# Constants awaited in parts, expert units of the first and last passes at other places, and a last sum on the vector engine, in a Mamba block between two expert layers

## The chip, the cores and the metric

One core of one Trainium2 chip runs the kernel. The metric is the time of one execution on the device in microseconds (us), the median of three runs. The five engines have their own instruction streams and meet through semaphores only: TensorE (PE; its weight loads are PEld), VectorE (DVE), ScalarE (ACT), GpSimd (POOL) and SyncE (SP), which here only issues DMAs.

## What is computed

32 sequences of 256 tokens with 128 channels pass through a half-weighted expert layer, a Mamba layer and a second half-weighted expert layer, each on a normalised input and added to the residual:

```python
x = x + 0.5 * ffn(layernorm(x))      # 8 experts of 176, top 2 of 8, and a shared expert of 352
x = x + mamba(layernorm(x))
x = x + 0.5 * ffn(layernorm(x))      # the same weights
# mamba, on r = layernorm(x):
xz = r @ W_in + b_in;  x_in, z = split(xz)                    # 256 each
xc = silu(causal_conv4(x_in) + conv_b)
Bm, Cm = split(xc @ W_xp + b_xp);  delta = softplus(xc @ W_dt + b_dt)
h_t = exp(delta_t * A) * h_(t-1) + delta_t * xc_t * Bm_t      # 256 channels x 16 states
y = sum over states of h_t * Cm_t + D_skip * xc
out = layernorm_std(r + (y * silu(z)) @ W_out + b_out)
```

## The kernel before, in words

**Tiles.** The 16 groups (`G`) are two sequences each, 512 tokens (`TG`). Channels lie on the 128 partitions in the Mamba part, so that one state of one group is one scan of 128x1024: `hist` from `decay` and the input term in the PSUM tile `ps_db`, 16 scans (`NS`) to a group, 256 in all (L924). GpSimd multiplies each with the row of C (`prod`, L623), and an accumulating DMA (L640) adds each pair of products to `yacc`; a last one, `fold` (L598), adds its two halves.

**The expert layer** is one pass of 14 units (`NCHUNK`): three of the shared expert (`ORDER` puts them first), then eleven of 128 rows of the experts. A unit is two up matmuls (`ps_h1` L1076, `ps_h2` L1098), a silu on ScalarE (L706), a multiply on VectorE (the gate, L904, with the row of routing weights `wrow` for expert units), a multiply on GpSimd for expert units (the join, L555), and four slots later (`BACK`) its down matmuls into `ps_y` (L1090). Up to seven gated tiles, four silus and four rows of weights are kept; the two PSUM tiles of each kind hold two units. The weight rows go by DMA through DRAM (`store_w`, then two DMAs of SyncE per unit, L418).

**Iterations.** The program is a pipeline over `k` from -2 to 17. Iteration `k` has 32 slots (`SLOTS`). Where group `k` exists, it runs its 16 scans, one per two slots, and beside them the first expert layer of group `k+2`, the front of the Mamba layer of group `k+1` (`lead`: `addy0` to `du`, ending in `bT`, the transposed B rows), the tail of group `k-1` (`fold`, the gating of y, the output projection, the layer norm `stats3` to `ln_add`, the routing of the second expert layer) and the second expert layer of group `k-2`. So iterations 2 to 13 hold 28 units each, iterations 0, 1, 14 and 15 hold 14, and -2, -1, 16 and 17 hold 14 units and no scan.

**What sets the order.** Tables written by hand: `PLAN` gives the slot of each step, `UNIT` the slots of the units, `SP_PLAN` the DMAs of SyncE; `START_PLAN`, `START_UNIT` and `START_SP` do so for `k` below 2 (`FULL`). Each engine walks the same slots and emits its own part of each step, so an engine's instructions stand in slot order and wait in that order. All the small matmul outputs (`xT`, `logits`, `wT`, `in0` to `in3`, `dt`, `xproj`, `cT`, `bT`, `outproj`) share one PSUM bank, `ps_m`, one after the other: a step waits until the one ahead has been copied out.

**Setup.** TensorE first waits for all eight expert weight loads, issued by ScalarE's queue (`experts_loaded`). SyncE issues the first group's x, fifteen constants (`consts_loaded`) and four more x. `prepare()` (VectorE, slot 24 of iteration -2) waits for all fifteen constants; `make_the_rest()` (GpSimd, slot 16) makes eleven small constants, `sel_b` among them, which the row broadcast `row_b` (L1058) needs; `make_edge()` (TensorE, slot 28) makes the edge term of the convolution.

## Time and profile before

| | before |
|---|---|
| median of 3 runs (lowest to highest) | 1839.37 us (1837.52 to 1846.04) |
| the profiled execution | 1839.04 us |
| its span, first to last instruction | 1837.3 us |
| PE / DVE / ACT / POOL busy | 1658.7 / 1478.3 / 1266.2 / 1445.7 us |
| mean granted TensorE clock | 0.959 |
| first matmul / first scan / last scan begin | 18.39 / 133.44 / 1740.03 us |

Busy shares are means over stages with different limits. The start, the sixteen scanning iterations and the end have to be read apart, which the windows do: each gives the busy time of every engine in one stretch.

### The profile page before, as it was taken

The page shows a single profiled execution, that of the slowest core. Times are in us where ns is not written, and L with a number is a line of the kernel's source. Part 1 is how long each engine was busy: PE and PEld are TensorE (multiplying, and loading weights), DVE is VectorE, ACT ScalarE, POOL GpSimd, SP SyncE. Part 2 cuts the span into 40 slices and gives each one's busy share as a digit, 9 for nine tenths or more (in the row PEclk, how much of TensorE's full clock was granted, in tenths as well). Part 3 has the DMA queues.
Part 4 walks back from the last instruction along what each step waited for, and adds up shares of the span by engine and source line. Part 5 has one row for each costly group of instructions (what it writes and reads, how often), then busy time and mean ns, then how long its engine had stood idle before and what let it go on. Part 6 is the DMA issues. An engine that isn't in the chain of part 4 may idle for free.

```text
span 1837.3 us, 24041 instructions
## 1 busy us (share of the span) xinstructions
PE 1658.7 (90%) x7378; PEld 1001.5 (55%) x7378; DVE 1478.3 (80%) x2241; ACT 1266.2 (69%) x2030; POOL 1445.7 (79%) x1366
## 2 busy tenths in 40 slices
PE   5898788999999999999999999999999999958488
PEld 3454445556555555656555555656555555534255
DVE  1438889989798988989798988989898998989732
ACT  2367678787877778776867777786877777665422
POOL 3336869888898988888888888888898888887753
PEclk9998889999999999999999999999999999969599
DMA  6026768687776868686777867777677868767642
GB/s 158 24 87 141 180 150 193 160 205 173 185 184 162 207 156 201 158 194 170 178 184 170 201 158 189 181 187 184 168 190 172 196 156 192 184 152 186 143 104 69
DMA packets 121287, 304.54 MB, mean 166 GB/s; under 512 B 19299, under 2 KB 40518, under 8 KB 106822
## 3 DMA queue, kind: packets, MB, share of 16 engines
q0 software_dynamic: 18432, 125.84, 34.4%
q1 hardware_dynamic: 98406, 174.46, 33.3%
q10 hardware_dynamic: 4320, 2.71, 0.5%
q8 instruction: 58, 0.95, 0.2%
q14 instruction: 71, 0.58, 0.1%
HBM read 167.67 MB, written 5.24 MB: 94 GB/s over the span
## 4 chain that ended last, share of the span: by engine, by line
POOL 43%; DMA 23%; issue 14%; PE 9%; DVE 7%; ACT 1%; SPq 1%; POOLq 0%; ACTq 0%; DVEq 0%
DMA yacc<-prod 19%; POOL prod L623 18%; POOL gated L555 14%; DVE hist L924 4%; DMA crow<-c_rows 3%; POOL yacc L619 2%; PE ps_y L1090 2%; DVE ps_db L876 2%; POOL yacc L640 1%; PE ps_h1a L1076 1%; SPq L418 1%; PE ps_h2a L1098 1%; PE ps_h1b L1076 1%; PE ps_h2b L1098 1%; POOL xres L610 1%
## 5 line engine op out<-in xcount | busy, mean ns | idle before, releaser
L623 POOL TENSOR_TENSOR prod<-hist,crow 128x1024 f32<-128x1024 f32 x224 | 556.5, 2484 | 204.7 <-DVE hist L924 171.0
L1090 PEld LDWEIGHTS ps_y<-down_w,gated 128*128 128x128 f32 (+1 forms) x3584 | 474.0, 196 | 276.4 <-issue 160.1
L924 DVE TENSOR_TENSOR_SCAN hist<-decay,ps_db 128x1024 f32<-128x1024 f32 x256 | 583.3, 2278 | 2.8
L555 POOL TENSOR_TENSOR gated<-gated,silu 128x512 f32<-128x512 f32 x352 | 493.3, 1450 | 74.4 <-DVE gated L904 71.4
L1090 PE MATMUL ps_y<-down_w,gated 128*128 128x128 f32 (+1 forms) x3584 | 491.8, 282 | 58.0 <-POOL gated L555 56.3
L876 DVE TENSOR_TENSOR ps_db<-du,ps_db 128x1024 f32<-128x1024 f32 x256 | 313.2, 1224 | 114.2 <-PE ps_db L1058 112.1
L686 ACT ACTIVATE decay<-delta,a_neg 128x510 f32<-128x510 f32 x512 | 326.8, 709 | 3.7 <-DVE delta L965 2.2
L706 ACT ACTIVATE silu<-ps_h1a 128x512 f32<-128x512 f32 (+1 forms) x224 | 132.9, 593 | 194.8 <-PE ps_h1a L1076 194.6
L1076 PE MATMUL ps_h1b<-xnT,up_w 128*128 128x512 f32 x448 | 236.7, 610 | 3.6 <-ACT silu L706 3.1
L1098 PE MATMUL ps_h2a<-xnT,up_w 128*128 128x512 f32 (+1 forms) x448 | 236.1, 609 | 1.9 <-DVE gated L904 1.9
L1076 PE MATMUL ps_h1a<-xnT,up_w 128*128 128x512 f32 (+1 forms) x448 | 236.4, 609 | 0.0
L1098 PE MATMUL ps_h2b<-xnT,up_w 128*128 128x512 f32 x448 | 232.0, 600 | 1.4 <-DVE gated L904 1.4
L904 DVE TENSOR_TENSOR gated<-ps_h2b,wrow 128x512 f32<-128x512 f32 x192 | 130.7, 681 | 60.3 <-PE ps_h2b L1098 40.2
L706 ACT ACTIVATE silu<-ps_h1b 128x512 f32<-128x512 f32 x224 | 133.0, 594 | 63.6 <-PE ps_h1b L1076 52.1
L686 ACT ACT_TABLE_LOAD x124 | 159.1, 1283 | 2.2
L904 DVE TENSOR_TENSOR gated<-ps_h2a,wrow 128x512 f32<-128x512 f32 x160 | 107.9, 674 | 46.3 <-PE ps_h2a L1098 36.2
L706 ACT ACT_TABLE_LOAD x111 | 142.4, 1283 | 2.0
L1058 PE MATMUL ps_db<-bT,sel_b 96*128 96x512 bf16 x256 | 102.2, 399 | 41.5 <-DVE hist L924 41.4
L1047 PE MATMUL ps_m<-xnT,w_conv 128*128 128x512 f32 (+3 forms) x256 | 118.2, 596 | 0.0
L1076 PEld LDWEIGHTS ps_h1a<-xnT,up_w 128*128 128x128 f32 (+1 forms) x448 | 85.0, 192 | 56.6 <-issue 47.0
L1076 PEld LDWEIGHTS ps_h1b<-xnT,up_w 128*128 128x128 f32 x448 | 79.1, 194 | 64.0 <-issue 37.5
L640 POOL DMA_DIRECT2D yacc<-prod x112 | 101.6, 908 | 1.6 <-issue 1.3
(136 smaller groups left out, 1937.5 us busy)
## 6 DMA issues: line engine op xcount, KB each, us to landing
yacc<-prod POOLq DMA_DIRECT2D x112, 1024.0 KB, 10.0
crow<-c_rows SPq DMA_DIRECT2D x128, 512.0 KB, 5.0
wrow<-w_rows SPq DMA_DIRECT2D x320, 128.0 KB, 6.3
wrow<-w_rows SPq DMA_DIRECT2D x64, 224.0 KB, 7.0
wrow<-w_rows SPq DMA_DIRECT2D x64, 192.0 KB, 6.4
wrow<-w_rows SPq DMA_DIRECT2D x64, 160.0 KB, 2.9
yacc<-yacc POOLq DMA_DIRECT2D x16, 512.0 KB, 7.8
wrow<-w_rows SPq DMA_DIRECT2D x64, 96.0 KB, 2.9
```

The costliest lines, as they stand in the source:

```text
L555: nc.gpsimd.tensor_tensor(gated[:, pos % NGATE, :], gated[:, pos % NGATE, :], silu[:, (pos + NCHUNK * f_parity(of, f)) % NSILU, :], ALU.mu ...
L623: nc.gpsimd.tensor_tensor(prod[:, (pair - 1 + odd) % 2, s % 2, :, :], hist[:, s % 2, :, :], c_all, ALU.mult).then_inc(prod_done, 1)
L640: pool.dma_start(yacc[odd][:], prod[:, (pair - 1 + odd) % 2, :, :, :], accum_op=ALU.add).then_inc(acc_done, 16)
L686: ins = nc.scalar.activation(decay[:, s % NA, half, :, 1:LEN], d[:, :, 1:LEN], ACT.Exp, scale=a_neg[:, half, s:s + 1])
L706: nc.scalar.activation(silu[0:r, (pos + NCHUNK * f_parity(k, f)) % NSILU, :], ps_h1[pos % 2][0:r, :], ACT.Silu).then_inc(silu_done, 1)
L876: nc.vector.tensor_tensor(ps_db[:].rearrange("p (h t) -> p h t", h=HALVES), du[par][:], ps_db[:, TG:2 * TG].unsqueeze(1).to_broadcast([P, ...
L904: nc.vector.tensor_tensor(gated[0:r, pos % NGATE, :], ps_h2[pos % 2][0:r, :], factor, ALU.mult).then_inc(h2_taken, 1)
L924: nc.vector.tensor_tensor_scan(hist[:, s % 2, :, :].rearrange("p h t -> p (h t)"), decay[:, s % NA, :, :, :].rearrange("p h b t -> p (h b ...
L1047: nc.tensor.matmul(acc[:, :, late:LEN], w_conv[:, tap, half * P:(half + 1) * P], now[:, :, 0:LEN - late], start=(tap == PAD), stop=False)
L1076: nc.tensor.matmul(ps_h1[pos % 2][0:r, :], up_w[:, 0, j * P:j * P + r], xnT[f][:], start=True, stop=True).then_inc(h1_full, 1)
L1090: ins = nc.tensor.matmul(ps_y[:, t * C:(t + 1) * C], gated[0:rd, posd % NGATE, t * P:(t + 1) * P], down_w[0:rd, jd, :], start=(posd == 0 a ...
L1098: nc.tensor.matmul(ps_h2[pos % 2][0:r, :], up_w[:, 1, j * P:j * P + r], xnT[f][:], start=True, stop=True).then_inc(h2_full, 1)
```

## The change

The tables are split by iteration. `PLANS[k]`, `UNITS[k]` and `SP_PLANS[k]` hold iterations -2, -1, 0, 14 (`G - 2`), 15, 16 and 17; the others keep their tables. An entry `name@1` belongs to the next iteration's work, `(f, pos, 1)` likewise for a unit.

- *Constants.* TensorE no longer waits for all expert weights at its start. The gate weights are awaited at the first `logits0`, the shared up weights at unit 0, the experts' up weights at unit 3, the down weights at the first down matmul. SyncE, not ScalarE, issues the down weights, right behind the first x. Behind the up weights' arrival it issues the five constants of the convolution (`conv_loaded`), and the other ten only in slot 8, behind the rows of the first four experts. `prepare()` becomes three steps: `taps_w`, `taps_b` and, an iteration later, `bias_parts`. `make_sel` stands in slot 2 on GpSimd. A silu of one element on ScalarE (`warm`) comes ahead of everything.
- *First passes.* The first pass (group 0) takes one unit per slot from slot 6. The second (group 1) has units 0 to 5 in iteration -2, units 6 and 7 in iteration -1, and units 8 to 13 in slots 0 to 5 of iteration 0, whose own 14 units follow from slot 7. The front of group 0 begins in iteration -2.
- *Last passes.* The last three passes begin one iteration sooner: seven units of group 13's pass in iteration 14 and seven in 15, eight units of group 14's in 15 and six in 16, and all of group 15's in 16. `ln_scale`, `ln_shift` and `ln_add` of the last group share slot 7.
- *Last sum.* For the last group, the seventh accumulate and the fold are left out. VectorE adds the second half of `yacc` and the two last products itself (`sum`).

```diff
+    PLANS[-2] = {
+        0: ["stats0"], 1: ["scale0"], 2: ["make_sel", "norm0"], 4: ["xT0"], 5: ["logits0", "rcopy0"], 6: ["route0", "tilt0"],
+        7: ["weights0", "wT0"], 12: ["taps_w"], 13: ["taps_b"], 15: ["stats0@1"], 16: ["scale0@1"], 17: ["norm0@1"],
...
+    UNITS[-2] = {6 + pos: (0, pos) for pos in range(NCHUNK)}
+    UNITS[-2].update({s: (0, pos, 1) for pos, s in enumerate((21, 22, 24, 26, 28, 30))})
+    SP_PLANS[-2] = {
+        7: ["store_w0", "w0:0", "w0:1", "w0:2", "w0:3"], 8: ["consts", "load:1"], 10: ["w0:4", "w0:5", "load:2"],
...
+    UNITS[-1] = {2: (0, 6), 4: (0, 7)}
...
+    UNITS[0] = {pos - 8: (0, pos, -1) for pos in range(8, NCHUNK)}
+    UNITS[0].update({s: (0, pos) for pos, s in enumerate((7, 8, 10, 13, 15, 18, 21, 22, 23, 24, 25, 27, 29, 31))})
...
+    UNITS[G - 2] = {s: unit for s, unit in UNIT.items() if unit[0] == 1}
+    UNITS[G - 2].update({s: (1, pos, 1) for pos, s in enumerate((21, 23, 25, 28, 29, 30, 31))})
...
+    UNITS[G - 1] = {s: (1, 7 + pos) for pos, s in enumerate((0, 2, 4, 6, 8, 10, 12))}
+    UNITS[G - 1].update({s: (1, pos, 1) for pos, s in enumerate((21, 22, 24, 27, 28, 29, 30, 31))})
...
+    UNITS[G] = {pos - 8: (1, pos) for pos in range(8, NCHUNK)}
+    UNITS[G].update({11 + pos: (1, pos, 1) for pos in range(NCHUNK)})
...
             load(0, 0, 0)
-            sp.wait_ge(x_loaded, 16)
+            full = HS // P
+            const(down_w[:, ECHUNK:ECHUNK + full, :], Ws3[0:full * P, :].rearrange("(j p) c -> p j c", p=P), down_loaded)
+            const(down_w[0:LAST, NCHUNK - 1, :], Ws3[full * P:HS, :], down_loaded)
+            const(down_w[:, 0:ECHUNK, :], W3.rearrange("e h c -> (e h) c").rearrange("(j p) c -> p j c", p=P), down_loaded)
+            sp.wait_ge(up_loaded, 16 * N_UP)
...
-                            if s % 2:
+                            if s % 2 and not (final(k + 1) and pair == PAIRS):
                                 accumulate(k, odd, pair)
...
+            act.wait_ge(pads_zero, 1)
+            nc.scalar.activation(warm[:], decay[:, 0, 0, 0, 0:1], ACT.Silu)
...
+                        elif step == "sum":
+                            dve.wait_ge(acc_done, 16 * (PAIRS * it - 1))
+                            dve.wait_ge(prod_done, NS * it)
+                            y_all = yacc[nxt][:, 0, :, :].rearrange("p h t -> p (h t)")
+                            left = prod[:, (PAIRS - 1 + nxt) % 2, :, :, :]
+                            for n, term in enumerate((yacc[nxt][:, 1, :, :], left[:, 0, :, :], left[:, 1, :, :])):
+                                if n:
+                                    dve.wait_ge(summed, n)
+                                nc.vector.tensor_tensor(y_all, y_all, term.rearrange("p h t -> p (h t)"), ALU.add
+                                                        ).then_inc(summed, 1)
...
             pe.wait_ge(consts_made, MADE_FIRST)
-            pe.wait_ge(experts_loaded, 16 * N_EXPERTS)
...
+                        if n == 0:
+                            pe.wait_ge(shared_loaded, 16 * 2)
+                        if n == NCHUNK - ECHUNK:
+                            pe.wait_ge(up_loaded, 16 * N_UP)
```

TensorE around the first scans, before. `ps_db<-bT,sel_b` is the row broadcast ahead of a scan, `ps_h` a unit's up matmuls, `ps_y` its down matmuls, and `bparts` the transpose for `bT`:

```order
L1037 MATMUL ps_m<-ident_bf,bparts 96x128 x4
L1076 MATMUL ps_h1a<-xnT,up_w 128x512
L1090 MATMUL ps_y<-down_w,gated 128x128 x4
L1098 MATMUL ps_h2a<-xnT,up_w 128x512
L1076 MATMUL ps_h1b<-xnT,up_w 128x512
L1098 MATMUL ps_h2b<-xnT,up_w 128x512
L1076 MATMUL ps_h1a<-xnT,up_w 128x512
L1090 MATMUL ps_y<-down_w,gated 128x128 x4
L1098 MATMUL ps_h2a<-xnT,up_w 128x512
L1076 MATMUL ps_h1b<-xnT,up_w 128x512
L1098 MATMUL ps_h2b<-xnT,up_w 128x512
L1058 MATMUL ps_db<-bT,sel_b 128x512
```

The same place after:

```order
L1136 MATMUL ps_m<-ident_bf,bparts 96x128 x4
L1248 MATMUL ps_m<-xnT,w_in 128x512
L1194 MATMUL ps_y<-down_w,gated 128x128 x4
L1248 MATMUL ps_m<-xnT,w_in 128x512
L1194 MATMUL ps_y<-down_w,gated 128x128 x4
L1157 MATMUL ps_db<-bT,sel_b 128x512
L1178 MATMUL ps_h1a<-xnT,up_w 128x512
L1202 MATMUL ps_h2a<-xnT,up_w 128x512
L1178 MATMUL ps_h1b<-xnT,up_w 128x512
L1202 MATMUL ps_h2b<-xnT,up_w 128x512
L1157 MATMUL ps_db<-bT,sel_b 128x512
```

Four units' up matmuls stood between the transpose for `bT` and the first row broadcast; now two small input matmuls and two down groups do, and the units stand behind it.

VectorE behind the last scan (`hist`), before, down to the first step of the gating of y (`xconv,d_c,yacc`):

```order
L924 SCALAR_TENSOR_TENSOR hist<-decay,ps_db 128x1024
L904 TENSOR_TENSOR gated<-ps_h2a,silu 128x512
L904 TENSOR_TENSOR gated<-ps_h2b,silu 128x512
L904 TENSOR_TENSOR gated<-ps_h2a,silu 96x512
L904 TENSOR_TENSOR gated<-ps_h2b,wrow 128x512
L904 TENSOR_TENSOR gated<-ps_h2a,wrow 128x512
L904 TENSOR_TENSOR gated<-ps_h2b,wrow 128x512
L904 TENSOR_TENSOR gated<-ps_h2a,wrow 128x512
L985 SCALAR_TENSOR_TENSOR yacc<-xconv,d_c,yacc 128x512
```

And after:

```order
L1016 SCALAR_TENSOR_TENSOR hist<-decay,ps_db 128x1024
L996 TENSOR_TENSOR gated<-ps_h2a,wrow 128x512
L996 TENSOR_TENSOR gated<-ps_h2b,wrow 128x512
L996 TENSOR_TENSOR gated<-ps_h2a,wrow 128x512
L1090 TENSOR_TENSOR yacc<-yacc 128x1024
L1090 TENSOR_TENSOR yacc<-yacc,prod 128x1024 x2
L996 TENSOR_TENSOR gated<-ps_h2b,wrow 128x512
L1102 SCALAR_TENSOR_TENSOR yacc<-xconv,d_c,yacc 128x512
```

Seven gates stood there; now three gates, the three adds and one more gate stand there.

SyncE's queue behind the first store of routing weights (`w_rows`), before:

```order
L403 DMA w_rows<-bounce 8x512
L418 DMA wrow<-w_rows 64x512 x2
L418 DMA wrow<-w_rows 48x512
L418 DMA wrow<-w_rows 80x512
L418 DMA wrow<-w_rows 96x512
L418 DMA wrow<-w_rows 32x512
L418 DMA wrow<-w_rows 64x512 x2
L418 DMA wrow<-w_rows 16x512
```

And after:

```order
L548 DMA b_dt_c<-L_attn_b_dt 128x2x1
L548 DMA w_xp<-L_attn_W_xp 128x2x32
L548 DMA b_xp_b<-L_attn_b_xp 128x32
L548 DMA a_log<-L_attn_A_log 128x2x16
L548 DMA d_c<-L_attn_D_skip 128x2x1
L548 DMA b_out_r<-L_attn_b_out 3x128
L548 DMA w_out<-L_attn_W_out 128x2x128
L548 DMA alpha_b<-L_attn_alpha 128x128
L548 DMA beta_b<-L_attn_beta 128x128
L470 DMA xres<-L_attn_x 128x4x128
L512 DMA wrow<-w_rows 16x512
L512 DMA wrow<-w_rows 112x512
```

Before, the constants stood far ahead of this place. Now ten of them (`w_dt`, right ahead of the rows shown, and the nine at their top) stand behind the rows of the first four experts and ahead of the fifth's (the pair of 16 and 112 partitions), with the next group's x.

## Rows read from the trace of the kernel before

**Rows 1.** Windows: stretch; us; busy of PE, PEld, DVE, ACT, POOL; clock, DMA share, GB/s.
```profile
18.39:133.40 115.01, 103.66 (x415) 60.66 (x415) 35.82 (x97) 50.91 (x87) 44.41 (x49) 0.94 0.23 68
133.40:217.60 84.20, 66.26 (x253) 37.68 (x252) 72.40 (x86) 64.11 (x94) 61.49 (x51) 0.88 0.65 157
217.60:311.90 94.30, 75.42 (x296) 44.84 (x297) 82.44 (x125) 67.53 (x111) 75.73 (x74) 0.87 0.69 163
415.70:520.40 104.70, 100.10 (x463) 60.79 (x462) 92.30 (x140) 79.11 (x128) 89.60 (x85) 1.00 0.75 180
1561.90:1654.20 92.30, 70.27 (x302) 42.06 (x301) 80.56 (x102) 61.62 (x94) 77.26 (x68) 0.84 0.70 167
1654.20:1740.00 85.80, 56.33 (x216) 33.37 (x215) 72.28 (x84) 45.76 (x71) 66.88 (x59) 0.76 0.71 169
1740.00:1837.30 97.30, 83.85 (x369) 52.06 (x367) 31.19 (x70) 24.19 (x48) 41.79 (x44) 0.90 0.35 87
```

**Rows 2.** Chain of waits, start of the program: start us, us, what.
```profile
7.30 11.00 DMA down_w<-L_ffn_W
18.39 1.10 PE ps_m L1037 x4
```

**Rows 3.** Timeline, ScalarE: start us, us, engine, line, operation [idle before <- releaser].
```profile
7.85 1.28 ACT L673 ACT_TABLE_LOAD   x1 [7.85 <-POOL nbias L544]
9.14 1.65 ACT L673 ACTIVATE xn<-xres,nbias,rstd 128x128 f32<-128x128 f32 x4
```

**Rows 4.** Chain of waits, first expert pass.
```profile
38.19 1.96 POOL sel_b L509
...
52.22 6.07 issue
```

**Rows 5.** Timeline, around the first scan.
```profile
131.28 0.38 PE L1058 MATMUL ps_db<-bT,sel_b 96*128 96x512 bf16 x1
...
133.44 2.28 DVE L924 TENSOR_TENSOR_SCAN hist<-decay,ps_db 128x1024 f32<-128x1024 f32 x1
```

**Rows 6.** Chain of waits, last expert pass, at full clock.
```profile
1808.76 0.86 PE ps_h1a L1076 x2
1809.62 0.89 PE ps_y L1090 x8
```

**Rows 7.** Timeline, SyncE's queue: first and last of ten constants' loads.
```profile
7.66 0.50 SPq L448 DMA_DIRECT2D w_dt<-L_attn_W_dt  x1
...
14.44 0.43 SPq L448 DMA_DIRECT2D beta_b<-L_attn_beta  x1
```

**Rows 8.** Tile wrow, VectorE: what its gate multiplies waited for (us, times).
```profile
  DMA wrow<-w_rows: 30.1, 19
```

**Rows 9.** Timeline, end of the last scans.
```profile
1740.03 2.29 DVE L924 TENSOR_TENSOR_SCAN hist<-decay,ps_db 128x1024 f32<-128x1024 f32 x1
...
1745.72 0.89 POOL L640 DMA_DIRECT2D yacc<-prod  x1 [0.25 <-POOL carrier_p L632]
...
1761.17 0.75 DVE L985 SCALAR_TENSOR_TENSOR yacc<-xconv,d_c,yacc 128x512 f32<-128x512 f32 x1 [3.73 <-DMA yacc<-yacc]
```

**Rows 10.** Line 969, an operation with both inputs in SBUF: ns min/median/max.
```profile
L969 DVE TENSOR_TENSOR du<-delta,xconv x16: 1198/1968/2976, 121.2 to 1647.5; 128x1024 f32<-128x1024 f32 x16
```

**Rows 11.** Chain of waits, from output projection to last expert pass.
```profile
1768.24 0.70 DVE rtok L917
...
1790.55 0.20 DVE logit L944
...
1794.95 1.71 PE ps_h1a L1076 x2
```

**Rows 12.** Page, parts 5 and 6: groups of instructions and DMA issues.
```profile
L623 POOL TENSOR_TENSOR prod<-hist,crow 128x1024 f32<-128x1024 f32 x224 | 556.5, 2484 | 204.7 <-DVE hist L924 171.0
...
L555 POOL TENSOR_TENSOR gated<-gated,silu 128x512 f32<-128x512 f32 x352 | 493.3, 1450 | 74.4 <-DVE gated L904 71.4
...
wrow<-w_rows SPq DMA_DIRECT2D x320, 128.0 KB, 6.3
```

758 lines of the change are left out of this document (405 added, 353 removed), and 23 rows, old and new, of the table SP_PLANS.

## The prediction

> **What bounds the kernel now.** I read the windows of busy time first, cut at the starts of the scans [rows 1]. Each stretch from 133.40 to 1740.00 us is one iteration of 16 scans, and the row for 415.70 to 520.40 stands for the twelve full ones, iterations 2 to 13: 104.7 us, in which TensorE is busy 100.1 at a granted clock of 1.00. The full iterations are bound by TensorE. Those at the ends are not: iteration 0 takes 84.2 us with TensorE busy 66.3 and VectorE 72.4, iteration 14 takes 92.3 with 70.3 and 80.6, iteration 15 takes 85.8 with 56.3 and 72.3. They have room on TensorE. Before the first scan lie 133.4 us, after the start of the last one 97.3 us, and there it is TensorE again, on the expert layers [rows 1]. So the ends have matrix work with no scan beside it, and the iterations next to them have scans with too little matrix work. The span is 1837.3 us, the execution 1839.04; the 1.7 us around it stay.
>
> The chain of waits says what else the ends hold. The first matmul starts at 18.39 us, released by the last of the weight loads, issued at 7.30 [rows 2]; the normalised rows it transposes were ready at 10.8, after a table load of 1.28 [rows 3]. In the first expert pass a 2 us piece of making `sel_b` on GpSimd stands in the chain (the last of three, behind a memset), and later 6.07 us of "issue" while VectorE works on the prepared constants [rows 4].
>
> **Start, to the first matmul.** PE now waits for the 14 small constants and the norm; the gate weights are awaited at `logits0`, the others where first read. ACT issues five loads and not eight, so its queue is free before the norm's inputs come, and the table load is done while it waits. With the norm's four activations (1.65) following at about 7.5, PE starts at 9.2: 9.2 us earlier, with 1.3 of it from the table. The down weights go out on the other queue at the same time as the up weights; they are 0.9 MB of the 2.7 MB that landed by 18.4 and are read only four units later, so I take no wait for them. If I am wrong on that, the first matmuls stall until what used to be 18.4, and at most 5 of the 9.2 are lost, since five units' work then lies ahead of them.
>
> Here a page speaks against it. The table switch took 1.28 us in the trace, and the ACTIVATE follows 0.01 behind it [rows 3]. The Trainium skill, ScalarE: Activation LUTs, section "What ACT_TABLE_LOAD costs", gives 1.283 us plus a drain of 1.38, about 2.66 per switch. After the change four switches lie between `sp_exp` and the first decays; by the page each would cost an estimated 1.38 us more than in the row, 5.5 in all, and the kernel would take 1820. The row has no such gap, and the sum goes by the row.
>
> **Start, to the first scan.** I count the work in PE's list. Before, between the first matmul and the first row broadcast (`row_b`, 131.28, [rows 5]), it holds 28 pairs of up matmuls and 24 groups of down matmuls: all 14 units of two passes. After, it holds 22 pairs and 22 groups, since six units of the second pass now come behind `row_b`. A matmul pair is 0.86 us, two to a unit, and a down group 0.89 at full clock [rows 6]: 6 x 1.72 + 2 x 0.89 = 12.1 us less. PE was busy 103.7 of the 115.0 us from 18.39 to 133.40 [rows 1], of which some 1.9 are behind `row_b`; that leaves 103.7 - 1.9 - 12.1 = 89.7. The idle part was 11.3. The `sel_b` stall (GpSimd now makes it in slot 2, between the norm and the first weights, where it waits) and the constants' stall (two short steps now, with the output bias put behind `du`) go, about 4 and 5 us. New idle comes: the rows of expert 4 stand on the SP queue behind ten constants, whose issue took 7.2 us (7.66 to 14.87, [rows 7]; 1 us left over on PE); the second pass's first three units fill only part of the wait for addy0, stats2, scale2 and norm2 (3 us); `dt0`, `dt1`, `xproj`, `cT`, `bT`, `in2`, `in3` pass through the one bank `ps_m` with fewer units between them, each waiting for ScalarE's copy (5 us); and ScalarE ends with `in3`, a table load and two decays after `row_b` (3 us, where the first scan stood 2.2 us behind `row_b` [rows 5]). So 12 us idle including that end, less clock saved by shorter gaps, which I take as 5 us of the lower 0.94 grant: 9.2 + 89.7 + 12 - 5 = 106. **First scan at 106 us, 27.4 earlier**; with the stalls halved or doubled, and none or all of the clock, 99 to 114.
>
> **The units that move into scans.** What a unit costs inside an iteration is read from two rows: iteration 1 has 14 units in 94.3 us and a full one 28 in 104.7, with the same tail and front steps [rows 1], so (104.7 - 94.3) / 14 = 0.74 us each, which is about one gate multiply on VectorE. Iteration 0 gets six more (20 units), iteration 14 seven more (21), iteration 15 one more (15). At 0.74 that is 4.4, 5.2 and 0.7. The other bound is the whole 2.61 us of PE work per unit [rows 6] where PE is late: 15.7, 18.3, 2.6. I take values near the lower end because PE has 18 to 30 us free in each, and add for placement. In iteration 0 six units come one per slot in the first three scans, about 5.8 us of PE work per scan against an average spacing of 84.2 / 16 = 5.3. In iterations 14 and 15 the rows for the moved units are stored right behind `next_c0` or `c7` on the SP queue, and a gate that waits for a row has a scan behind it on VectorE; the whole run had only 30.1 us of that wait in 19 places [rows 8]. **+6.5, +6 and +2 us.** Iterations 1 to 13 have the same list on each engine; +0.
>
> **The end.** Before, the last accumulate is issued at 1745.72, the fold behind it, and the gating of y starts at 1761.17, which is 21.1 us after the last scan began at 1740.03 [rows 9]. After, VectorE adds three 128x1024 tensors itself. Such an add with both inputs in SBUF took 1.20 at least, 1.97 in the middle and 2.98 at most [rows 10]: 3.6 to 8.9, taken as 5.9, since GpSimd still multiplies beside it. The sixth accumulate has landed by about +5, since the seventh could be issued at 1745.72. But `sum` stands behind three unit gates (positions 6 to 8), and their matmuls begin on PE only behind the last row broadcast, two units and a half of 2.61 us and more at the lower clock: it starts at +7.5, ends at +13.4, and the four multiplies of the y gates (0.75 each at least, [rows 9]) with two unit gates take about 7 us if they too are held up: +20.5. The output projection then ends at +23, against 1768.24, that is +28.2 [rows 9, 11]: 5.2 us won of the 16 that the accumulate and the fold held.
>
> From there to the logits' arrival on VectorE took 22.3 us (1768.24 to 1790.55) [rows 11]. The layer norm's three GpSimd multiplies no longer have unit multiplies between them: 2.2 less. The units now start behind the logits and not behind the routing: 1790.55 to 1794.95, 4.4 us [rows 11], less 0.7 for the transpose that they now carry. The expert rows then come at about +13 after the logits where PE wants them at +11; the two-deep buffers take that up. Sum: 5.2 + 2.2 + 3.7 = 11.1, **end 11 us shorter**, with 6 to 15 as bounds (the adds at 8.9 and a stall on the rows; the adds at 3.6).
>
> **Sum.** 1839.0 - 27.4 + 6.5 + 6 + 2 - 11.1 = 1815.0 us. The profiled execution is 0.3 us below the median of the three runs, so this stands for the median too.
>
> **Rivals.**
> (a) *The moved units hide better, and PE runs without the clock losses.* Their low price holds (10.3 instead of 14.5), the first scan comes at 101, the end is 13 shorter: 1839 - 32.4 + 10.3 - 13 = 1804. For it: 18 to 30 us of free TensorE time. Against: VectorE is at 72 to 81 of 84 to 92 us there.
> (b) *The iterations that receive them behave like full ones, or worse.* Then iterations 0 and 14 go towards 100 and 104, +16 and +12, and 15 +4, first scan at 108: 1839 - 25 + 32 - 11 = 1835; in its milder half, 1827. For it: GpSimd multiplies 1.45 us per expert unit beside its 2.48 per scan [rows 12], and the accumulate DMA chain paces iteration 0.
> (c) *Slower: rows late in front of scans.* Fifteen units with expert rows are gated in iterations 0, 14 and 15 in places of the scans where none was. If each gate waits for its row, the scan behind it is held. A row's landing took 6.3 us in the median [rows 12]. The change decides for slower from a mean wait of 24 / 15 = 1.6 us; at half a landing, 3.1 us, it costs 47 and gives 1862. Against it: 19 waits in 352 such gates before.
> (d) *The start does not do what it says*: weights shared over two queues land no earlier and PE stands at 18 as before. First scan 9 later, 1824; it lies in the range.
>
> A second rule bears on the end. Adds of this form took between 1.20 and 2.98 us [rows 10]. The Trainium skill, SBUF — State Buffer, section "Who interferes with whom", has a VectorE instruction with two SBUF inputs fully blocked while a GpSimd one that reads SBUF runs. By it, each of the three adds could stand behind a whole multiply, an estimated 7 to 9 us for the sum, and the kernel 1 to 3 us later than the forecast, inside the range.
>
> **How the numbers follow.** The forecast, 1815, has 0.56; (a) 0.20; (b) 0.19; (c) 0.05; (d) is a part of the forecast's spread. The range takes in the forecast with its own bounds (about 1805 to 1826), most of (a) below and the milder half of (b) above: 1800 to 1830. A measurement of this kernel can tell some 0.5% from no change, 9 us. Faster by more is below 1830: the forecast, (a), and two thirds of (b), 0.89. Within 0.5%: the rest of (b) and a little of (c), 0.08. Slower: 0.03.
>
> **What would show it.** In the profile after: the first matmul at 9 to 10 us; no `sel_b` in the chain; the first scan at 99 to 114; iterations 0, 14 and 15 at 90.7, 98.3 and 87.8; the twelve full ones unchanged; three adds on VectorE at 1.2 to 3 us each, starting 7 to 8 us after the last scan's start; 86 us from there to the end. It is wrong if the first matmul waits for a weight, if gates wait on `wrow` for far over 30 us in all, if TensorE's grant in iteration 0 falls further below 0.88, or if full iterations change though their lists do not.

## The result, and the profile after

The changed kernel takes **1854.37 us** (median of 9 runs, 1849.88 to 1857.21), the kernel before 1840.83 (9 runs, 1834.86 to 1846.04). The ratio is 1.0074, with a 95% interval of 1.0059 to 1.0088: slower by 0.7%. The forecast was 1815.0 with a range of 1800 to 1830, so the time lies outside it and on the other side of no change. The profiled execution has a span of 1851.0 us, 13.7 more than the 1837.3 of before.

The windows of busy time, cut at the starts of the scans as in [rows 1], say where they are. Columns: stretch in us; its length; busy time of PE, PEld, DVE, ACT and POOL with their instructions; granted clock, DMA share, GB/s.

```profile
9.39:102.63 93.24, 86.28 (x365) 52.42 (x366) 33.65 (x92) 37.41 (x72) 34.32 (x36) 0.98 0.35 96
102.63:210.37 107.74, 79.30 (x311) 43.86 (x309) 74.43 (x91) 75.99 (x109) 68.21 (x57) 0.92 0.53 133
210.37:303.24 92.87, 78.18 (x288) 46.00 (x289) 80.95 (x125) 66.21 (x108) 74.77 (x74) 0.80 0.71 165
1555.82:1677.64 121.82, 95.17 (x362) 55.56 (x361) 83.60 (x109) 71.47 (x107) 80.09 (x72) 0.82 0.58 142
1677.64:1767.09 89.45, 53.83 (x206) 31.09 (x206) 72.36 (x84) 43.83 (x69) 64.59 (x56) 0.79 0.68 156
1767.09:1851.00 83.91, 69.24 (x318) 45.22 (x317) 33.52 (x68) 18.50 (x39) 41.02 (x39) 0.91 0.22 67
```

Beside the forecast's terms (us; an iteration runs from the start of its first scan to the next iteration's):

| stretch | before | after | difference | forecast |
|---|---|---|---|---|
| first matmul | 18.4 | 9.4 | -9.0 | -9.2 |
| start to first scan | 133.4 | 102.6 | -30.8 | -27.4 |
| iteration 0 | 84.2 | 107.7 | **+23.5** | +6.5 |
| iteration 1 | 94.3 | 92.9 | -1.4 | 0 |
| iterations 2 to 13 | 1250.0 | 1252.5 | +2.5 | 0 |
| iteration 14 | 92.2 | 121.9 | **+29.7** | +6 |
| iteration 15, to the last scan | 85.8 | 89.4 | +3.6 | +2 |
| last scan to the end | 97.3 | 83.9 | -13.4 | -11.1 |
| sum | 1837.3 | 1851.0 | +13.7 | -24.0 |

(The first row is part of the second.) The start and the end gained more than forecast. Two iterations lost 53 us where 12.5 had been expected: iteration 0, with 20 units, is longer than a full iteration with 28 (103 to 107), and iteration 14, with 21 units, is the longest of the run.

How far such a length can be read is seen from the experiments below, since many of them share tables. The ten profiles with the changed kernel's tables for iteration 14 gave 119.8 to 121.9 us for it; the seven with its tables for iteration 0 gave 107.7 to 109.8; the stretch after the last scan gave 83.9 to 85.7, the first scan 101.9 to 104.7, and the twelve full iterations together 1247 to 1254. Differences under 2 us in one stretch (3 at the first scan) are not read as effects. Only `e1`, `e2`, `e5`, `e11` and `e16` were executed more than once (4 to 10 times); each of the others is one execution, and is read by its stretches.

**The start** did what it was to do. The timeline, ScalarE and TensorE (start, length, engine, line, operation; in brackets the idle time before it and what ended it):

```profile
3.35 1.28 ACT L758 ACT_TABLE_LOAD   x1 [3.35 <-issue]
4.64 0.20 ACT L758 ACTIVATE warm<-decay 128x1 f32<-128x1 f32 x1
7.60 1.65 ACT L771 ACTIVATE xn<-xres,nbias,rstd 128x128 f32<-128x128 f32 x4 [2.75 <-POOL nbias L645]
```
```profile
9.39 1.09 PE L1136 MATMUL ps_m<-ident,xn 128*128 128x128 f32 x4 [9.39 <-ACT xn L771]
```

The table load of [rows 3] lies ahead of the norm, TensorE starts on the norm and not on a weight as in [rows 2], and the two stalls of [rows 4] are gone from the chain.

**Iteration 14** shows two long waits of VectorE, each with a scan behind it. Its timeline:

```profile
1606.01 2.28 DVE L1016 TENSOR_TENSOR_SCAN hist<-decay,ps_db 128x1024 f32<-128x1024 f32 x1
1615.55 0.06 DVE L950 MEMSET carrier_s<- 128x1 f32 x1 [7.26 <-POOL xres L710]
...
1618.46 2.28 DVE L1016 TENSOR_TENSOR_SCAN hist<-decay,ps_db 128x1024 f32<-128x1024 f32 x1
...
1633.18 1.23 DVE L971 TENSOR_TENSOR ps_db<-du,ps_db 128x1024 f32<-128x1024 f32 x1 [4.69 <-PE ps_db L1157]
...
1659.71 1.20 DVE L1071 TENSOR_TENSOR du<-delta,xconv 128x1024 f32<-128x1024 f32 x1
1669.34 0.69 DVE L996 TENSOR_TENSOR gated<-ps_h2b,wrow 128x512 f32<-128x512 f32 x1 [8.42 <-DMA wrow<-w_rows]
```

The first: the statistics of the second norm (`stats1`) now stand in slot 17 with the layer norm's last add (`ln_add`), which GpSimd reaches behind two unit multiplies and a scan product; the scan of slot 18 waits behind them, 12.5 us from one scan to the next. The last: the first gate that reads a row of routing weights waits 8.4 us for it, again with a scan behind it. SyncE's queue at that place:

```profile
1644.98 0.32 SPq L486 DMA_DIRECT2D c_rows<-bounce  x1
1658.57 0.32 SPq L491 DMA_DIRECT2D crow<-c_rows  x1
1658.94 0.46 SPq L497 DMA_DIRECT2D w_rows<-bounce  x1
```
```profile
1653.89 0.59 ACT L846 ACTIVATE bounce<-ps_m 8x512 f32<-8x512 f32 x1 [1.19 <-PE ps_m L1136]
```

ScalarE had the weights in `bounce` by 1654.5. Their store (`w_rows<-bounce`) went out at 1658.94, behind the load of the next group's first C rows (`crow`), which waits for the products of scan 13.

**Iteration 0** has the same two kinds. Its longest gap, 13.9 us from scan 6 (141.27) to scan 7 (155.16), on VectorE and TensorE:

```profile
141.27 2.29 DVE L1016 TENSOR_TENSOR_SCAN hist<-decay,ps_db 128x1024 f32<-128x1024 f32 x1
149.37 1.23 DVE L971 TENSOR_TENSOR ps_db<-du,ps_db 128x1024 f32<-128x1024 f32 x1 [5.81 <-PE ps_db L1157]
154.55 0.69 DVE L996 TENSOR_TENSOR gated<-ps_h2b,wrow 128x512 f32<-128x512 f32 x1 [3.96 <-DMA wrow<-w_rows]
155.16 2.28 DVE L1016 TENSOR_TENSOR_SCAN hist<-decay,ps_db 128x1024 f32<-128x1024 f32 x1
```
```profile
143.72 1.09 PE L1136 MATMUL ps_m<-ident,x1n 128*128 128x128 f32 x4 [4.06 <-ACT bounce L846]
144.59 1.92 PE L1178 MATMUL ps_h1b<-xnT,up_w 128*128 128x512 f32 x2
146.30 1.10 PE L1202 MATMUL ps_h2b<-xnT,up_w 128*128 128x512 f32 x2
147.23 1.88 PE L1146 MATMUL ps_m<-xnT,w_conv 128*128 128x512 f32 x4
148.95 0.38 PE L1157 MATMUL ps_db<-bT,sel_b 96*128 96x512 bf16 x1
```

The row broadcast for scan 7 (`ps_db<-bT,sel_b`, 148.95) stands on TensorE behind the transpose of the second norm, and that waits for ScalarE. In the kernel before this chain stood in slots 5 to 8; it could not stay there, because the six units of the second pass now end in slot 9 and the second norm needs their sum.

### The profile page after: what moved, and what is told of

The parts are those of the page before. It is cut to its first block, busy times and chain, and to the rows that moved or that the text cites. A ratio compares the mean times of both kernels' runs of the same rounds, so it can differ in the third digit from the quotient of the medians.

```text
span 1851.0 us, 24043 instructions
## 1 busy us (share of the span) xinstructions
PE 1665.0 (90%) x7378; PEld 1005.1 (54%) x7378; DVE 1484.5 (80%) x2244; ACT 1266.1 (68%) x2031; POOL 1445.5 (78%) x1362
## 4 chain that ended last, share of the span: by engine, by line
POOL 44%; DMA 17%; issue 15%; PE 14%; DVE 5%; ACT 4%; POOLq 0%; SPq 0%; DVEq 0%; ACTq 0%
POOL prod L723 18%; DMA yacc<-prod 15%; POOL gated L654 13%; PE ps_y L1194 4%; POOL yacc L719 3%; DVE hist L1016 2%; PE ps_h1a L1178 2%; PE ps_h2b L1202 2%; PE ps_h1b L1178 2%; PE ps_h2a L1202 2%; POOL yacc L740 2%; DMA wrow<-w_rows 1%; PE ps_m L1146 1%; DVE ps_db L971 1%; POOL xres L710 1%
## 5 line engine op out<-in xcount | busy, mean ns | idle before, releaser
L1202 PE MATMUL ps_h2b<-xnT,up_w 128*128 128x512 f32 x448 | 237.3, 612 | 9.5 <-DVE gated L996 9.4
L1157 PE MATMUL ps_db<-bT,sel_b 96*128 96x512 bf16 x256 | 101.7, 397 | 44.2 <-DVE hist L1016 44.0
L1178 PEld LDWEIGHTS ps_h1a<-xnT,up_w 128*128 128x128 f32 (+1 forms) x448 | 85.1, 193 | 62.5 <-issue 45.9
```

Source lines behind the costliest of these rows:

```text
L1178: nc.tensor.matmul(ps_h1[pos % 2][0:r, :], up_w[:, 0, j * P:j * P + r], xnT[f][:], start=True, stop=True).then_inc(h1_full, 1)
L1202: nc.tensor.matmul(ps_h2[pos % 2][0:r, :], up_w[:, 1, j * P:j * P + r], xnT[f][:], start=True, stop=True).then_inc(h2_full, 1)
```

## The experiments

**Theories.** U: the moved units make the two iterations long, by their work and their own waits. T: the steps that had to move with them do (router, norms, transposes), because in their new slots one engine waits for another with a scan queued behind it.

### One move undone at a time

`e1_late_back` puts the last passes back, `e2_first_back` the second pass and iteration 0 (here and below `...` stands for lines left out):

```
+    for table, full in ((PLANS, PLAN), (UNITS, UNIT), (SP_PLANS, SP_PLAN)):
+        table[G - 2] = table[G - 1] = full
...
+    UNITS[G] = {pos: (1, pos) for pos in range(NCHUNK)}
+    UNITS[G].update({16 + pos: (1, pos, 1) for pos in range(NCHUNK)})
...
```
```
+    UNITS[-1] = {1 + n: (0, 6 + n) for n in range(8)}
...
+    PLANS[0], UNITS[0], SP_PLANS[0] = START_PLAN, START_UNIT, START_SP
```

> The changed kernel with its last three expert passes put back: iterations 14 and 15 take the tables of the full ones again (14 units each), and all 14 units of the pass before the last stand behind the last scan, beside the sum and the output projection. The two profiles put +29.7 us on iteration 14 and +3.7 on iteration 15. Both theories expect iterations 14 and 15 at about 92 and 86 us, 33 shorter. What is open is the end (83.9 us in the changed kernel, 97.3 before): if its gain came from the chain (sum on VectorE, no multiplies between the layer norm's steps), it stays at 84 to 88 and the kernel takes about 1822; if it came from the eight units that no longer stand there, it goes back to 95 to 98 and the kernel takes 1832 to 1835.

> The changed kernel with the second pass's six units back ahead of the first scan and iteration 0 with its old tables (14 units, old steps); loads and the early front stay. Expected by both theories: first scan about 12 us later than 102.6, so near 115; iteration 0 back from 107.7 to 84 to 86; iteration 14 unchanged at about 122. Kernel about 1854 + 12 - 23 = 1843. If iteration 0 stays over 95, its length is not from its own tables but from what the start leaves behind (a colder clock, accumulates).

Measured: `e1_late_back` 1821.41 us, ratio to before 0.9907 (0.9890 to 0.9924). Iterations 14 and 15 took 91.5 and 85.8, and the end 87.6: with all 28 units behind the last scan it is still 9.7 shorter than before. The end's gain comes from its chain; moving eight units away from it was worth at most 4 us there (87.6, and 85.9 in a later kernel, against 83.9 to 85.7), and cost 34 in iterations 14 and 15. `e2_first_back` 1839.78 us, ratio 1.0011 (0.9999 to 1.0023): first scan at 116.0, iteration 0 at 85.9. The first move alone wins 13.4 and costs 21.8.

### Units against steps

`e3_first_units` takes the six units out of iteration 0 and leaves its other tables; `e4_late_units` takes the seven out of iteration 14:

```
+    UNITS[-1] = {1 + n: (0, 6 + n) for n in range(8)}
...
+    UNITS[0] = {s: unit for s, unit in UNITS[0].items() if len(unit) == 2}
...
```
```
+    UNITS[G - 2] = {s: unit for s, unit in UNIT.items() if unit[0] == 1}
+    UNITS[G - 1] = {pos: (1, pos) for pos in range(NCHUNK)}
+    UNITS[G - 1].update({s: (1, pos, 1) for pos, s in enumerate((21, 22, 24, 27, 28, 29, 30, 31))})
...
```

> As the run before, but iteration 0 keeps the changed kernel's order of steps and the places of its own 14 units; only the six moved units are gone from it. Theory U (the units' work and their waits beside the scans make iteration 0 long): iteration 0 falls from 107.7 to under 90 us. Theory T (the steps are squeezed: the norm, the router and the input matmuls of the group stand in neighbouring slots, and one engine waits for another inside a scan's slot): it stays over 98 us, since those steps stand as they did. First scan near 115 either way.

> The changed kernel with iteration 14 freed of the seven units of the pass begun early, its steps left where the changed kernel has them (statistics in the slot of the layer norm's last add, router five slots earlier). The seven units go to iteration 15, which then has 22. Theory U: iteration 14 falls from 121.9 to under 97 us, near the 92.3 of before. Theory T: it stays over 108, since 7.3 us of waiting for the layer norm's add and the half clock behind it do not depend on the units. Iteration 15 gets longer by 5 to 18 us, the end stays at 84.

Iteration 0 fell only to 102.5, as theory T has it. With the same 14 units, the old tables take 85.9 and the new ones 102.5, so **16.6 us come with the new tables** and 5.2 with the six units, 0.87 each. The new tables move the steps most, but also nine of the iteration's own 14 units, by one to three slots, and with them the loads of their rows; no run moves these units alone. What VectorE waited for in iteration 0, `e2_first_back` and then `e3_first_units` (us, times, longest):

```profile
DVE ps_db L975 <- PE ps_db L1161: 7.4, 6, 2.6
```
```profile
DVE ps_db L976 <- PE ps_db L1162: 27.0, 11, 6.4
DVE gated L1001 <- DMA wrow<-w_rows: 3.7, 1, 3.7
```

Iteration 14 fell to 103.3, between the two expectations. Its 14 units stand there in their old slots, so 11.1 us are the steps (the wait for the layer norm's add stayed at 7.2), and **18.6 the seven units**, 2.7 each. (The router's steps stand two to four slots earlier there, not five.) Iteration 15, with 22 units and not 15, took 102.7 and not 89.4: 1.9 for each of the seven.

### The queue of the weight rows

`e9_rows_first` puts the store of the weights and the first rows ahead of the load of C rows in iteration 14:

```
-        26: ["next_c0"], 27: ["store_w1", "w1:0", "w1:1", "w1:2", "w1:3"],
+        26: ["c_put"], 27: ["store_w1", "w1:0", "w1:1", "next_c0", "w1:2", "w1:3"],
```

(`c_put` is the store of the C rows, split from their load.)

> The changed kernel with one change to SyncE's queue in iteration 14: the store of the routing weights and the rows of the first two experts go ahead of the load of the next group's first C rows, which waits for the products of scan 13. In the changed kernel the weights lay ready at about 1654.5, the store went out at 1658.94, and the first gate with a row waited 8.4 us with scan 14 behind it. If that queue is the cause, the wait falls to 3 to 5 us, the 14.2 us from scan 14 to scan 15 fall to about 10, and iteration 14 gets 4 us shorter. If the rows' own landing is the cause, nothing moves.

Iteration 14 went to 114.2: 7.7 us shorter than in the changed kernel, and at least 5 shorter than in any other with its tables. SyncE's queue, and what VectorE then waited for:

```profile
1651.62 0.29 SPq L503 DMA_DIRECT2D w_rows<-bounce  x1
1653.12 2.19 SPq L518 DMA_DIRECT2D wrow<-w_rows  x4
1655.69 0.34 SPq L497 DMA_DIRECT2D crow<-c_rows  x1
```
```profile
DVE gated L1004 <- DMA wrow<-w_rows: 3.3, 2, 2.8
```

The store goes out 6.1 us earlier in its iteration (at 97.0 us of it, not 103.2), and the longest wait of a gate for a row falls from 8.4 to 2.8. Scan 14 to scan 15 fell from 14.2 to 6.1 us. Of the units' 18.6 us this is 6 to 8, one wait, for the first row.

### Single chains shifted: the waits move on

`e8_stats_slot` puts `stats1` of iteration 14 into slot 18, behind the scan, with the following steps a slot later; `e7_norm_slot` puts the second norm of iteration 0 a slot earlier.

```
-        17: ["dt0", "ln_add", "stats1"], 18: ["dt1", "scale1"], 19: ["norm1"], 20: ["sp_exp", "xT1"],
+        17: ["dt0", "ln_add"], 18: ["dt1", "stats1"], 19: ["scale1"], 20: ["sp_exp", "norm1"], 21: [..., "xT1", ...],
```
```
-        9: ["addy0", "tilt0"], 10: ["weights0", "stats2", "scale2"], 11: ["norm2", "wT0"], 12: ["xT2"],
+        9: ["addy0", "stats2", "scale2", "tilt0"], 10: ["weights0", "norm2"], 11: ["xT2", "wT0"],
```

> The changed kernel with the statistics of the second norm in iteration 14 one slot later than the layer norm's last add (slot 18 and not 17, behind the scan), and norm, transpose and first unit of the last pass each a slot later. If the 7.3 us that VectorE stood on GpSimd's add with a scan queued behind it are the price of the shared slot, the 12.5 us from scan 8 to scan 9 fall to under 7, the half clock behind it (5.4 us without a matmul) goes or shrinks, and iteration 14 falls from 121.9 to 110 to 115. If another wait takes its place, iteration 14 stays over 118.

> The changed kernel with one chain of iteration 0 a slot earlier: statistics and scale of the second norm in slot 9, right behind the add of the expert output and ahead of the scan, the normalisation in slot 10, its transpose in slot 11. Units stay. If the 13.9 us from scan 6 to scan 7 come from that chain (statistics behind a scan, then GpSimd, ScalarE, the transpose on TensorE with the row broadcast of scan 7 queued behind it), that gap falls to 5 to 8 us and iteration 0 from 107.7 to about 100. If they come from the units' work, the gap stays or moves to the next scan and iteration 0 stays over 105.

Both missed. In `e8_stats_slot` scan 8 to scan 9 fell from 12.5 to 4.5 us as expected, but scan 10 to scan 11 rose from 12.2 to 16.3 and scan 9 to 10 from 4.2 to 7.4: iteration 14 took 119.4. The wait had gone to TensorE, and from there to the row broadcast:

```profile
1627.30 3.59 PE L1273 MATMUL ps_m<-w_xp,xconv 128*128 128x32 f32 x16 [4.26 <-ACT xnT L814]
```
```profile
1631.36 1.23 DVE L978 TENSOR_TENSOR ps_db<-du,ps_db 128x1024 f32<-128x1024 f32 x1 [10.07 <-PE ps_db L1164]
```

The transpose of the norm (slot 21) and `xproj` behind it use the one bank `ps_m`; ScalarE's copy out of it stood behind a table load and four decays, and the row broadcast of scan 11 behind `xproj`. In `e7_norm_slot` scan 6 to scan 7 fell from 13.9 to 8.8, scans 4 to 6 took 3.3 more, and iteration 0 stayed at 108.2.

Two further attempts had iteration 0 without the six units as their base (102.5). `e12_input_chain` put the second norm and two input matmuls back to their old slots, with the router left late; `e13_input_late` put the last two input matmuls in slot 19 and not 27 and 28.

> As the kernel with the six units gone from iteration 0 but its steps left late (iteration 0: 102.5 us), with one group of steps put back to its old slots: the add of the expert output, the second norm, its transpose and the two convolved input matmuls (slots 3 to 13 and not 9 to 16). The router, the last two input matmuls (slots 27 and 28) and the units stay late. If this chain carries most of the 16.6 us between 102.5 and 85.9, iteration 0 falls to 90 or below; if the router or the late input matmuls carry it, it stays over 96.

> As the kernel with the six units gone from iteration 0 and its steps left late (102.5 us), but the last two input matmuls, whose results ScalarE must copy from the one PSUM bank, stand in slot 19 and not in 27 and 28. If they hold the last scans, the 8.7 us from scan 14 to scan 15 fall to 5 to 6 and iteration 0 to about 99; if the waits there come from the three late units' joins (TensorE waited 2.4 us for one), the gap stays over 8.

They took 108.3 and 104.4. In the first, the transposes of router and second norm met in slots 6 and 7, and scan 3 to scan 4 rose from 7.0 to 11.6. In the second the last four scans did become shorter, from 30.4 to 24.2 us, and the six before them longer, from 39.5 to 48.1. So no step that was tried "costs" the 16.6 us by itself: a chain put among others moves the wait.

`e14_router_early` separates the two chains: the router ends in slot 9, ahead of the second norm. `e15_rows_first0` adds to it the order of the queue: the weights' store ahead of the fifth load of C rows.

```
+        4: ["xT0"], 5: ["logits0"], 6: ["rcopy0", "route0"], 7: ["tilt0"], 8: ["weights0"], 9: ["wT0", "addy0"],
+        10: ["stats2", "scale2"], 11: ["norm2"],
```
```
-        11: ["c4"], 12: ["store_w0", "w0:0", "w0:1", "w0:2"],
+        10: ["store_w0", "w0:0", "w0:1"], 11: ["c4"], 12: ["w0:2"],
```

> As the same kernel (102.5 us), but the router's steps end in slot 9, ahead of the second norm (transpose in slot 4, logits 5, weights 8, their transpose 9), which stays late in slots 10 to 12. Before, TensorE waited 4.1 us for ScalarE's copy of the routing weights, which stood behind the normalisation, and the row broadcast of scan 7 stood behind that. If this meeting of the two chains is the cause, the 13.7 us from scan 6 to scan 7 fall to about 8 and iteration 0 to about 96. If the second norm alone is enough to hold the scan, the gap stays over 12.

> As the kernel with the router early in iteration 0 (96.8 us), but the store of the routing weights and the first two experts' rows stand ahead of the fifth load of C rows on SyncE's queue, which waits for the products of a scan. If the queue's order is what the gate waited for, the 4.3 us of waiting for rows go, the gap from scan 6 to scan 7 falls from 14.1 to about 10 and iteration 0 to about 93. If the landing of the rows is what it waited for, the gap stays.

`e14_router_early`: iteration 0 at 96.8, as expected, but not for the expected reason. Scan 6 to scan 7 stayed at 14.1 us, so the second norm alone holds that scan; the gain came from scans 3 to 5 (14.2 to 11.0) and 12 to 15 (25.8 to 22.0). `e15_rows_first0`: scan 6 to 7 fell from 14.1 to 10.6, VectorE waited for no row any more in the iteration, and it took 93.6. The wait for rows before, `e14_router_early`:

```profile
DVE gated L1005 <- DMA wrow<-w_rows: 4.3, 1, 4.3
```

Of the 16.6 us, 5.7 went with the router's earlier slots and 3.2 with the queue's order (one execution each, against a spread of 2 us). 7.7 are left. The largest piece visible of these is scan 6 to scan 7, 10.6 us against 4.9 in `e2_first_back`; what the changed places of the iteration's own units have in it stays open.

### The start and the end by themselves

`e10_all_loads` makes TensorE wait for all expert weights before its first matmul; `e6_fold` gives the last sum back to the seventh accumulate and the fold.

```
+            for loaded, parts in ((wg_loaded, 1), (shared_loaded, 2), (up_loaded, N_UP), (down_loaded, N_DOWN)):
+                pe.wait_ge(loaded, 16 * parts)
```
```
-        1: ["sum"], 2: ["gate_y0"], 3: ["gate_y1"], 4: ["outproj"], ...
+        1: ["fold"], 2: ["gate_y0"], 3: ["gate_y1"], 4: ["outproj"], ...
```

> The changed kernel with TensorE waiting for all expert weights before its first matmul, as the kernel before did; queues, norm and table load stay in their new places. The prediction had 9.2 us from the first matmul and took all of it through to the first scan. Expected: first matmul at 16 to 18.4 and not 9.4, first scan 6 to 9 us later than 102.6, the rest unchanged. If the first pass has slack, or later waits (the rows, GpSimd's joins) set its pace, the first scan moves by less than 4.

> The changed kernel with the last sum given back to the seventh accumulate and the fold; all else as it is. The prediction had the sum on VectorE save 5.2 us of the end: the end goes from 83.9 to 89. Rival: the wait for the accumulate and the fold is covered by the six units that stand there, and the end stays within 2 us of 83.9; or the adds on VectorE hardly save anything since they run beside GpSimd's multiplies and hold the gates back.

`e10_all_loads`: first matmul at 13.56, not 16 to 18.4.

```profile
13.56 1.09 PE L1139 MATMUL ps_m<-ident,xn 128*128 128x128 f32 x4 [13.56 <-POOL sel_b L614]
```

(The releaser named there is a neighbour in time: TensorE waited for no piece of `sel_b`. SyncE, which waits for the up weights before its next load, issues that at 13.23.) The first scan came at 106.9, 4.3 later for a matmul 4.2 later, and later than in all kernels with the same start: against the 101.9 to 104.7 us of those kernels that is 2.2 to 5.0 later, so half or more of what is won at the first matmul arrives at the first scan, and perhaps all. Both missed the expectation. Of the 9.0 us, 4.2 are the waiting in parts; the other 4.8 came with the new queues, with all weights there by 13.5 and not 18.4. Two things changed in them at once: SyncE took over the down weights, and its fifteen constants, which it issued from 4.00 to 14.87 before, now wait for the up weights. No run separates the two.

`e6_fold`: the end took 91.6 us, where 89 had been expected, and not 83.9, so the sum on VectorE is worth 7.7, or 6 by the longest end of the other kernels. Against the changed kernel's adds, the fold that VectorE waited for:

```profile
1786.03 0.75 DVE L1104 SCALAR_TENSOR_TENSOR yacc<-xconv,d_c,yacc 128x512 f32<-128x512 f32 x1 [9.44 <-DMA yacc<-yacc]
```
```profile
1767.10 2.28 DVE L1016 TENSOR_TENSOR_SCAN hist<-decay,ps_db 128x1024 f32<-128x1024 f32 x1
...
1773.78 1.56 DVE L1090 TENSOR_TENSOR yacc<-yacc 128x1024 f32<-128x1024 f32 x1
1775.38 4.38 DVE L1090 TENSOR_TENSOR yacc<-yacc,prod 128x1024 f32<-128x1024 f32 x2
```
```profile
1786.11 2.05 PE L1280 MATMUL ps_m<-w_out,yacc 128*128 128x128 f32 x16
```

### Versions that beat both kernels

`e5_both_back` undoes both moves and keeps the rest. `e11_spread` adds two small moves to it; `e16_mended` keeps the six units in iteration 0 and mends the router and the queue there.

> The changed kernel with both moves of expert units undone: the second pass stands ahead of the first scan, the last passes where they stood, iterations 0, 14 and 15 by the old tables. What stays: loads in parts, the early front, the sum on VectorE, the tighter chain at the end. From the runs before: 1821.4 with the last passes back; undoing the first move makes the first scan 13.4 us later (116.0 against 102.6) and iteration 0 21.8 shorter (85.9 against 107.7), so 8.4 less: 1813, some 1.5% faster than the kernel before. If the two moves are not independent, it comes out elsewhere than 1810 to 1816.

> The kernel with both moves undone (1810.3), with two edits that squeeze no step. First, two of the six units (the last two of the second pass) stand in slots 0 and 1 of iteration 0, and only the add of that pass moves, from slot 3 to 5. Second, in iterations 14 and 15 the 14 units lie over slots 0 to 20 and not 0 to 17, since TensorE is busy 47.2 of 48.0 us in the first half of iteration 14 and 23.0 of 44.2 in the second. Theory: a moved unit is cheap where no chain is shortened for it: first scan 4 us earlier (112), iteration 0 up by under 2 (87), iterations 14 and 15 shorter by 2 to 4 each; kernel about 1803. Rival: any unit beside scans costs its 2.6 us or more: iteration 0 at 91, iterations 14 and 15 as they were, 1811.

> The kernel with the last passes back (1821.4 us; six units moved, first scan 102.5, iteration 0 109.7), with two mends in iteration 0: the router's steps end in slot 9 and not 11, and the routing weights' store stands ahead of the fifth load of C rows. If both mends carry over from the runs without the units (8.9 us), iteration 0 takes 99 to 101 and the kernel about 1812: no better than with the units ahead of the first scan (1810). If the units eat the mends, as when one chain was shifted by a slot, iteration 0 stays over 105 and the kernel takes 1817 or more.

| kernel | us | ratio to before (95%) | first scan | it. 0 | it. 14 | it. 15 | end |
|---|---|---|---|---|---|---|---|
| changed | 1854.37 | 1.0074 (1.0059 to 1.0088) | 102.6 | 107.7 | 121.9 | 89.4 | 83.9 |
| `e1_late_back` | 1821.41 | 0.9907 (0.9890 to 0.9924) | 102.5 | 109.7 | 91.5 | 85.8 | 87.6 |
| `e5_both_back` | 1810.26 | 0.9857 (0.9841 to 0.9873) | 116.5 | 85.5 | 92.1 | 85.8 | 85.9 |
| `e11_spread` | 1811.53 | 0.9857 (0.9829 to 0.9885) | 111.1 | 89.0 | 91.7 | 88.9 | 87.6 |
| `e16_mended` | 1815.05 | 0.9858 (0.9832 to 0.9884) | 102.2 | 99.9 | 91.7 | 86.7 | 86.0 |

The ratio is the column to compare, since each was taken against the kernel before on the same chip and these differ by some us. `e5_both_back` is 1.4% faster than the kernel before, with a plain order. In `e11_spread` the two units cost 3.5 us in iteration 0 for 5.4 at the first scan, so the pair gains 1.9, too little to be told from nothing; spreading the units of iterations 14 and 15 gained nothing and cost 3.1 in iteration 15. The kernel came out where the rival had it (1811) and not at the 1803 of the theory. In `e16_mended` both mends carried over to the kernel with the units: 109.7 to 99.9, inside the 99 to 101 expected. First scan and iteration 0 together then take 202.1, against 202.0 in `e5_both_back`, 200.1 in `e11_spread` and 210.3 in the changed kernel. Mended, the move of the six units breaks even; it wins nothing.

## Why the prediction was wrong

**The start: right.** First matmul 9.4 (forecast 9.2). First scan 102.6 (106, 99 to 114). Split: the six units out of the way were worth 13.4 (forecast 12.1), everything else 17.4 (15.3). TensorE was busy 86.3 us from the first matmul to the first scan and idle 7.0; the forecast had 84.7, with the clock, and 12. The fear that the down weights come late did not show.

**The end: right, with two sizes off.** The three adds took 5.9 us as forecast and began 6.7 after the last scan's start (7.5). The output projection ended at 21.1 (23). The sum was worth 6 to 7.7, not 5.2: without it VectorE waits 9.4 us for the fold. The end came out at 83.9 (86.2).

**Iteration 15: near**, +3.6 for +2.

**Iterations 0 and 14: wrong, and this decides.** The step that failed is "The units that move into scans". It read a price of 0.74 us per unit as the difference between iteration 1 and a full one, "with the same tail and front steps", and used it where the steps are not the same. The two rows were not alike in the clock either: iteration 1 had a grant of 0.87, the full ones 1.00 [rows 1], so the price can hold a gain of clock, and iteration 14 got none (0.82 after, 0.84 before). For the six units of iteration 0 alone it was sound: 5.2 us measured, 0.87 each, against the 6.5 forecast with placement. For the seven of iteration 14 it was not: 18.6 us, 2.7 each, for +6. The **steps that move with the units were priced at nothing**, though the tables of the diff show them: in iteration 0 the second norm goes from slots 5 to 7 to slots 10 to 12 and its input matmuls crowd into 13 to 16; in iteration 14 the norm, transpose, logits and weights go two to four slots earlier and `stats1` into the slot of `ln_add`. They cost 11.1 us in iteration 14. In iteration 0 the new tables cost 16.6, of which 8.9 went when only the router's slots and the queue's order were changed.

The argument of "18 to 30 us of free TensorE time" failed with it. The free time was real, but it lay in the second half of iteration 14: in the kernel before, TensorE was busy there 23.0 of 44.2 us, and half of its idle time was row broadcasts waiting for a scan (`hist`, 10.4 us in four waits).

```profile
1610.00:1654.20 44.20, 22.98 (x96) 14.25 (x95) 36.70 (x48) 29.36 (x47) 36.01 (x33) 0.66 0.67 155
```

Units that stand there put their matmuls ahead of the row broadcasts. In the changed kernel TensorE stood 5.4 us for scan 9, which the layer norm's add had held back. Behind that its work took about twice as long: a pair of up matmuls 1.91 us, at the lower clock. So it was busy without a break from 1625.68 until the row broadcast of scan 11, the one for which VectorE waited 4.69 us:

```profile
1620.80 0.61 PE L1157 MATMUL ps_db<-bT,sel_b 96*128 96x512 bf16 x1 [5.39 <-DVE hist L1016]
...
1627.55 1.91 PE L1202 MATMUL ps_h2a<-xnT,up_w 128*128 128x512 f32 x2
1629.26 3.46 PE L1266 MATMUL ps_m<-w_xp,xconv 128*128 128x32 f32 x16
1632.53 0.61 PE L1157 MATMUL ps_db<-bT,sel_b 96*128 96x512 bf16 x1
```

With seven units and the early steps that half took 71.7 us, with TensorE busy 45.9:

```profile
1605.90:1677.60 71.70, 45.89 (x146) 26.25 (x145) 38.17 (x54) 37.22 (x58) 37.93 (x36) 0.69 0.49 122
```

No engine was near its limit in it. The price per unit there was 2.7, at the upper bound that the prediction had named (2.61) and turned down. The clock has a part in it that no run separates: the grant was 0.69 in that half, and eight of its sixteen pairs of up matmuls took 1.9 to 2.1 us, the lower of the two levels (1.2 GHz), where the shortest of 128 rows took 1.0.

**The rivals.** (b) had the right place and too little: +16, +12 and +4 for +23.5, +29.7 and +3.6, 32 of 56.8 us. It named GpSimd and the accumulates as the cause. GpSimd has a part: VectorE's 7.3 us in iteration 14 were for its add, which stood behind its multiplies, and TensorE waited 8.8 us for joins in iteration 0 (5.1 before). The accumulates show in none of the long waits of VectorE and TensorE. (c) had a right mechanism with the wrong shape. It priced a mean wait over fifteen gates; what came was one long wait in each iteration, for the first row, because the store behind it was queued behind a load that waits for a scan's product: 8.4 and 4.0 us, worth 6 to 8 in iteration 14 and about 3 in iteration 0. So the kernel came out slower, as (c) alone had it, but rows were only some 10 of the 56.8 us that the three iterations lost. In all, gates waited 41.4 us for rows, against the 30.1 of [rows 8]. The prediction looked at where rows stand on the queue behind `next_c0` and took it as a small addition. Of (a), the start and the end came true and the cheap units did not; (d) did not happen.

**Of the signs it named**, "gates wait on `wrow` for far over 30 us" came half; TensorE's grant in iteration 0 rose, from 0.88 to 0.92. Neither would have shown the largest wait, that of `ps_db` for the row broadcast. In iteration 0 it went from 5.5 us to 29.0 (us, times, longest; before, after):

```profile
DVE ps_db L876 <- PE ps_db L1058: 5.5, 6, 1.7
DVE ps_db L971 <- PE ps_db L1157: 29.0, 11, 5.8
```

In iteration 14 it went from 7.2 to 13.9, beside the waits of 8.4 and 7.3 us for the row and for GpSimd's add.

## What to carry to other kernels

When work moves into a stretch, write down which steps must move with it because they need its result or its buffer, and price them too: for each, the engine it waits for, and what is queued behind it there. Free time of an engine that waits for others is no room; look in which half of the stretch it lies and what ended it. On an in-order queue, a store that others wait for belongs ahead of a load that waits for compute.

A mend of one wait in a tightly packed order is to be measured on the whole stretch: four of the seven here moved the wait elsewhere and won under 3 us or lost.
